# Unit-matrix products on TensorE ahead of its waits, in ten turns of a twelve-sublayer decoder

## What is computed

```
x = _layernorm(x + _L0_attn_ref(x, ...))    # linear attention
x = _layernorm(x + _L0_xattn_ref(x, ctx))   # cross attention, one head
x = _layernorm(x + _L0_ffn_ref(x, ...))     # mixture, 8 experts, top 2, capacity
x = _layernorm(x + _L1_attn_ref(x, ...))    # local and compressed global attention
x = _layernorm(x + _L1_xattn_ref(x, ctx))   # cross attention with a side bias
x = _layernorm(x + _L1_ffn_ref(x, ...))     # linear with an 8 bit rounding
x = _layernorm(x + _L2_attn_ref(x, ...))    # long convolution, as matrix products
x = _layernorm(x + _L2_xattn_ref(x, ctx))   # random-feature attention
x = _layernorm(x + _L2_ffn_ref(x, ...))     # mixture, 15 experts, top 3
x = _layernorm(x + _L3_attn_ref(x, ...))    # grouped attention with a norm inside
x = _layernorm(x + _L3_xattn_ref(x, ctx))   # sigmoid attention, normed q and k
x = _layernorm(x + _L3_ffn_ref(x, ...))     # a two-layer local transformer
```

## Time and profile before

| | before |
|---|---|
| median of three timed runs | 2589.14 us (2584.22 to 2590.63) |
| the profiled execution's own time | 2594.83 us |
| its span, first to last instruction | 2593.1 us |
| PE busy | 2218.9 us, 86% of the span |
| PE weight loads | 1613.4 us, 62% |
| DVE, ACT, POOL busy | 54%, 41%, 28% |
| mean granted TensorE clock | 0.924 of full speed |

### The profile page before, as it was taken

The page is one execution under the profiler, slowest core; times in us unless marked ns, Lnnn a source line. Parts: engine busy times, 40 slices in busy tenths (PEclk is TensorE's granted clock), DMA queues, the critical chain, the costliest instruction groups (busy, mean ns, idle before and its releaser), DMA issues. The chain is left out here.

```text
span 2593.1 us, 37797 instructions
## 1 busy us (share of the span) xinstructions
PE 2218.9 (86%) x12776; PEld 1613.4 (62%) x12776; DVE 1409.6 (54%) x4103; ACT 1060.4 (41%) x2653; POOL 723.4 (28%) x738
## 2 busy tenths in 40 slices
PE   7993599888869959995699799687899799899898
PEld 5772377665547648883388566354465587465687
DVE  3664122256658947757133567544777443777455
ACT  3542111135516620055034166343567543567532
POOL 2323311110004414411634200363534200534111
PEclk9995799979959979996899899899999899999899
DMA  9132211085000010030254301401000000000000
GB/s 235 43 146 103 75 51 44 14 168 43 1 7 1 1 43 1 19 135 7 92 151 129 128 18 29 169 1 33 1 1 1 1 1 1 1 1 1 21 25 21
DMA packets 112237, 127.32 MB, mean 49 GB/s; under 512 B 46515, under 2 KB 100021, under 8 KB 110256
## 3 DMA queue, kind: packets, MB, share of 16 engines
q1 hardware_dynamic: 103312, 103.91, 14.9%
q0 software_dynamic: 8736, 20.99, 2.2%
HBM read 79.93 MB, written 47.90 MB: 49 GB/s over the span
## 5 line engine op out<-in xcount | busy, mean ns | idle before, releaser
L461 PE MATMUL bank<-weights,work 128*128 128x256 f32 (+5 forms) x1768 | 452.4, 393 | 18.8 <-DVE weights L2552 8.1
L461 PE MATMUL bank<-work,weights 128*128 128x256 f32 (+2 forms) x1552 | 392.8, 404 | 19.3 <-DVE work L4794 12.1
L461 PEld LDWEIGHTS bank<-weights,work 128*128 128x128 f32 (+2 forms) x1768 | 318.4, 191 | 101.1 <-issue 49.6
L461 PEld LDWEIGHTS bank<-work,weights 128*128 128x128 f32 x1552 | 293.5, 194 | 91.0 <-DVE work L4794 16.2
L845 POOL TENSOR_TENSOR work<-work,minus_half 128x2 f32<-128x2 f32 x96 | 69.3, 722 | 705.9 <-DVE work L838 705.9
L461 PE MATMUL bank<-weights,x_feat 128*128 128x512 f32 (+2 forms) x576 | 213.6, 505 | 14.8 <-ACT weights L4398 9.1
L870 ACT COPY x_feat<-bank 128x512 f32<-128x512 f32 x80 | 46.6, 585 | 301.8 <-PE bank L862 301.8
L461 PEld LDWEIGHTS bank<-weights,x_feat 128*128 128x128 f32 x576 | 107.4, 199 | 71.8 <-issue 45.9
L4422 ACT ACTIVATE work<-work 128x128 f32<-128x128 f32 (+1 forms) x256 | 137.1, 545 | 0.2
L461 PE MATMUL bank<-x_feat,weights 128*128 128x256 f32 (+3 forms) x400 | 117.7, 472 | 22.1 <-PEq L247 15.2
L1785 DVE TENSOR_TENSOR work<-bank,work 128x384 f32<-128x384 f32 (+1 forms) x64 | 31.4, 491 | 190.6 <-ACT work L1703 190.6
(11 more groups left out here) (461 smaller groups left out, 4503.6 us busy)
## 6 DMA issues: line engine op xcount, KB each, us to landing
weights<-in_weights SPq DMA_DIRECT2D x1, 12296.0 KB, 33.1
weights<-in_weights SPq DMA_DIRECT2D x1, 9360.0 KB, 25.7
weights<-in_weights SPq DMA_DIRECT2D x1, 8488.0 KB, 23.1
work<-rows_in SPq DMA_DIRECT2D x62, 129.0 KB, 2.2
rows_in<-ident SPq DMA_DIRECT2D x2, 3968.0 KB, 43.1
weights<-rows_back SPq DMA_DIRECT2D x8, 768.0 KB, 4.9
work<-rows_in SPq DMA_DIRECT2D x8, 645.0 KB, 4.2
rows_in<-ident SPq DMA_DIRECT2D x2, 2560.0 KB, 33.5
```

The source lines that it names most:

```text
L461: ins = nc.tensor.matmul(out, lhsT, rhs, start=(i == 0), stop=(i == len(pairs) - 1))
```

## The change

A new helper issues a given number of products of the unit matrix with itself into the first 128 columns of a PSUM bank that nothing holds at that moment. It is called in ten turns: once in each mixture, there behind a new PE wait for the semaphore that counts the scattered rows, and at chosen steps of the loops of the other turns.

```diff
+def keep_busy(nc, K, bank, calls):
+
+    for _ in range(calls):
+        nc.tensor.matmul(bank[:, 0:P], K.ident[:], K.ident[:], start=True, stop=True)
@@ mixture_top2
             pe.wait_ge(S.slot_done, 1)
+            pe.wait_ge(K.scattered_top2, 16 * TOP * TILES)
+            keep_busy(nc, K, K.bank[0], 10)
             for j in range(PARTS[0][2]):
                 turn_row(j)
@@ local_global_attention
             for t in range(STEPS):
+                keep_busy(nc, K, K.bank[X], {0: 4, 4: 5}.get(t, 0))
@@ side_attention
             for t in range(STEPS):
+                keep_busy(nc, K, K.bank[Z], {0: 4, 1: 3, 2: 4}.get(t, 0))
@@ mixture_top3
             pe.wait_ge(S.table_done, 1)
+            pe.wait_ge(K.scattered_in, 16 * TOP * TILES)
+            keep_busy(nc, K, K.bank[0], 10)
@@ grouped_attention
             for t in range(STEPS):
+                keep_busy(nc, K, K.bank[0], {2: 10, 3: 5, 4: 6, 5: 4, BACK + 26: 16, BACK + 30: 20}.get(t, 0))
@@ sigmoid_attention
             for t in range(STEPS):
+                keep_busy(nc, K, K.bank[Z if t < LEAD + 1 else 0],
+                          {1: 5, 4: 5, 5: 4, 6: 5, 7: 4, 8: 4, BACK + 31: 14}.get(t, 0))
@@ local_attention (both layers)
             for t in range(STEPS):
+                keep_busy(nc, K, K.bank[X], {0: 7, 2: 8, 3: 3}.get(t, 0))
@@ local_ffn (both layers)
                 if (b := at_step(t, HT, B)) is not None:
                     mean(b)
+                keep_busy(nc, K, K.bank[Y], {0: 4, 2: 6, LEAD: 15}.get(t, 0))
                 if (n := at_step(t - LEAD, 1, CHUNKS)) is not None:
                     hidden(n)
```

## The result

The changed kernel takes 2568.49 us in the median of 7 runs (2564.36 to 2578.48), the kernel before 2587.53 us beside it. The ratio is 0.9931, 95% interval 0.9921 to 0.9942: 18 us less, 15 to 20. Two later measurements of the same kernel gave 0.9930 (0.9912 to 0.9947) and 0.9930 (0.9912 to 0.9948). The profiled execution spans 2568.8 us.

A forecast was written before the change was run, and what follows sets the result against it. PE, busy 86% of the span, was taken to set the pace, often at half clock just behind its waits. Place terms sum to 18.8 us less: 2589.1 - 18.8 = 2570.3 us, range 2559 to 2585.

The forecast's parts named there:

- Rival (a): All places with calls: calls do not raise or hold the clock, only overhang; 17.5 us more, 2606.6 us; 5%.
- Rival (b): Local and global, side attention: clock rises no earlier in the two longest half-clock stretches; sum 8.1, 2581.0 us; 12%.
- Rival (c): DVE, ACT and POOL become late once PE is fast; half the gross gain lost, 9 to 10 us, 2580 us; 12%.
- Rival (d): Whole kernel: falls of the clock just move elsewhere; a sum within 5 us, 2588 us; 6%.
- first local attention: Start of the first layer's local attention: first steps at full clock save 2.6 us, less 0.45 overhang; 2.15 us less.
- the feed-forwards: Both feed-forward parts: half-clock stretches behind the calls run at full clock; net 2.7 and 1.6 us less.
- Local and global attention: Its start: 6.2 us from full clock, less 1.7 and 0.8 overhang and 0.7 for ACT and DVE; net 3.0 less.
- Side attention: Its start: 9.23 us of half-clock work gives 4.6, less 1.7 ahead of an unwaited projection; net 2.9 us less.
- Grouped end and sigmoid: Grouped attention's end through sigmoid attention: 1.0 us net, then 2.0 with POOL making powers late; together 3.0 us less.
- Grouped start: Start of grouped attention: projection and most transposes at full clock, calls ending 2.0 us late; net 0.5 us less.
- First mixture: Ten calls fill the row load, nothing late; the half-clock stretch behind runs at full clock, 3.1 us less.
- Second mixture: Ten calls make PE's first rows 2.1 us late, full clock returns 2.4; net 0.3 us less.

The follow-up runs named there:

- e3: Changed kernel with each call issued as two transposes of the unit matrix instead of one product; ratio 0.9916 to the kernel before.
- e4: Changed kernel with each call multiplying 32 rows of the unit matrix instead of 128; 2609.43 us, ratio 1.0076 to the kernel before.
- f4: Changed kernel plus eight calls in each of three waits at the mixtures' ends, minus the four starting local and global attention; 2568.88 us, ratio 0.9911.
- g1: Changed kernel with all edits that pointed down joined: calls added at mixture ends and other waits, calls cut ahead of unwaited projections; 2566.03 us, ratio 0.9901.
- g2: Changed kernel plus five calls ahead of the second scores of local and global attention, in their wait for DVE; 2569.98 us, ratio 0.9920.
- e2: Changed kernel with calls kept only in grouped, sigmoid and local attention and feed-forwards, without the added PE waits; 2579.85 us, ratio 0.9959.
- e1: Changed kernel with calls kept only in the two mixtures, local and global attention and side attention; 2582.85 us, ratio 0.9978.
- f2: Changed kernel with second mixture's calls cut 10 to 5, local attention's first group 7 to 5, 14 added before sigmoid's first projection; 2574.23 us, ratio 0.9926.

## Why the prediction was right, and where its terms were not

Forecast 18.8 us less and 2570.3 us; measured 0.69% and 2568.49 us. The mechanism was right, and e3 with e4 shows it from both sides: as many records in the same places, and only those behind which the clock is up bring the gain. Rival (a) is excluded for the change and true for 32 rows. Rival (b), that the clock does not rise sooner in the two longest stretches, is excluded: it was up at 545.0 and 753.2, ahead of both, though it fell again in the first. Rival (c), that other engines come last, is excluded as a general rule by the stretches that gained in full, but true for the start of grouped attention. Rival (d) is not the main effect but is real as a disturbance: see the stretches without calls in the table. That the sum came out so close is partly luck: local and global attention, grouped attention and the second mixture gave less than their terms, the first mixture, side and sigmoid attention more, and these misses nearly cancel.

Of the signs named, the projections behind two branches start later by 1.84 us (1.7 forecast), the first feed-forward's hidden products run wholly at full clock, and the second local attention's start is 0.5 us longer (0.4). The mean clock rose to 0.942, more than the 0.935 forecast, and the time at half clock fell by 93 us, not 60.

Terms right to 0.2 us in three profiles: first local attention (-2.15, measured -2.1), second (+0.45, +0.5), the feed-forwards (-2.7 and -1.6, measured -2.8 and -1.6). The pair in the earlier trace rows was the best evidence: the same code at both clocks.

Mis-sized terms:
- Local and global attention, forecast 3.0, measured 0.9, 0.6 and 2.0. The step that failed is the halving of 12.35 us of busy time, less 0.7: 5.5 us. 3.9 us of it are the compression, which takes as long at full clock (3.92 and 3.98 us for 16 records), so at most 4.2 us were to be had. Where the clock was at full throughout (the third profile, f4, g1, g2), the stretch from the first scores to 570.16 was 3.1 us shorter than before; in the first two profiles the clock fell back behind DVE's wait, for 6.8 us, and 1.7 us were left. The four and five calls made the first scores 0.8 to 1.1 us late, where I had taken 1.7 + 0.8. I had used this very row as a bound on the price of a call; at full clock a call costs 0.22 us (records of the helper start 0.112 us apart in the median), as taken from the other rows.
- Side attention, forecast 2.9, measured 3.8, 3.2 and 3.2. The clock rose during the first projection already, at 753.19, while I had counted only what lay in the stretch of the earlier trace rows, which begins behind it.
- Grouped end and sigmoid, forecast 3.0, measured 3.8 three times. POOL did not come last: the products from 1668.57 ran on to kv's with the 1.16 us wait that they had before, so the full 2.7 us of the second stretch arrived where I had taken 2.0.
- Grouped start, forecast 0.5, measured 0.0 three times, though its projection took 1.99 us in place of 3.78. The next products ended a wait for DVE (1.42 us before at 1487.21, 0.46 after) at the same distance from the turn's start as before: DVE came last there.
- First mixture, 3.1 against 3.9 to 4.2. From the rows to 296.87 it is 3.2 to 3.3 us, as forecast; the other 0.6 to 1.0 us come at its end, where there are no calls. Without calls (e2) it was 1.3 us shorter than before all the same.
- Second mixture, forecast 0.3 us less: measured 0.8 and 0.4 us more and 1.3 us less. The overhang was real, as the calls end 4.4 us after the scatter; the rest varies.

Not foreseen: the rest of either local attention, behind the turn's first transpose, changed by -1.5 in the first and by +2.6 or -1.3 in the second. The first (1.5 to 1.7) came in all eight profiles with the change's calls in that turn, and not in e1, e4 and f2. In the second layer the clock's falls come or stay away from one execution to the next. Such falls make the profiles' sums differ by 7 us where the sum of the ten places differs by 0.8. Why a given fall comes in one execution and not in the other is not settled; no run here separates it from the moment at which the program started.

## What to carry to other kernels

Look first at how much of TensorE's busy time lies at half clock just behind its waits; half of that is what filling can give, less what is bound otherwise, so check in a pair of rows whether the same code really runs faster at full clock. Fill a wait with products or transposes over all rows, sized by the wait divided by the call's full-clock time. Do not put calls ahead of work that waits for nothing: four such calls delayed it by 1.84 us. The waits at the end of the turn ahead served better here (f4, g1). Judge such edits place by place, since falls elsewhere move by several us and hide a gain of 2 us in the total.

## What was not expected of the hardware

- A transpose of a float32 128x128 matrix raises and holds the clock as a product does: ratio 0.9916 with transposes and 0.9931 with products.
- Products on 32 rows keep PE busy as long at the same clock (32 records in 3.83 us against 3.74 on 128 rows, at full clock), and yet the clock was down behind them where it was up behind 128 rows: mean clock 0.925 against 0.942, 40 records in 8.9 us against 4.6.
- A product whose x_feat operand is read at every fourth column takes the same at both clocks, 0.245 us a record of 128 columns, where one of the unit matrix takes 0.21 at half and 0.11 at full. That the stride is the cause is likely but was not tried alone.
